# Segment attention of an eight-layer model on one core: probabilities turned one unit later, next batch's projections in quarters

## The reference, cut to what matters

```python
x = x + _L1_attn_a_ref(_layernorm(x), Wq, bq, Wk, bk, Wv, bv, Wo, bo)

def _L1_attn_a_ref(x, Wq, bq, Wk, bk, Wv, bv, Wo, bo):
    H, DK, SEG, NN, DIL = 16, 8, 64, 2, 4
    def _attn(q, k, v):
        scores = jnp.einsum('bshqd,bshkd->bshqk', q, k) / math.sqrt(q.shape[-1])
        return jnp.einsum('bshqk,bshkd->bshqd', jax.nn.softmax(scores, axis=-1), v)
    q, k, v = proj_chunk(Wq, bq), proj_chunk(Wk, bk), proj_chunk(Wv, bv)   # (batch, segment, head, 64, 8)
    out = _attn(q, k, v)
    kd, vd = k[:, :, :, ::DIL], v[:, :, :, ::DIL]
    for off in range(1, NN + 1):
        for sign in (-1, 1):
            n = seg_ids + sign * off
            valid, nc = (n >= 0) & (n < S), jnp.clip(n, 0, S - 1)
            out = out + jnp.where(valid, _attn(q, kd[:, nc], vd[:, nc]) / (2 * NN), 0.0)
    return merge_heads(out) @ Wo + bo
```

## Time and profile before

| what | value |
|---|---|
| median of 3 runs | 1274.57 us |
| lowest and highest | 1271.35 and 1275.83 us |
| profiled execution, its own time | 1270.62 us |
| its span, first to last instruction | 1268.9 us |
| segment stage in it, first maximum of unit 0 to that of unit 63 | 824.80 to 1067.97 us |
| VectorE, ScalarE, GpSimd busy over the whole span | 73%, 65%, 16% |
| mean granted clock of TensorE | 0.968 |

### The profile page before, as it was taken

One profiled execution on the slowest core, in us unless ns is written; L12 is line 12 of the kernel. 1 busy time (PEld: TensorE's weight loads), 2 busy tenths in 40 slices (PEclk: granted clock), 3 DMA queues, 4 the chain that ended last, 5 costly groups with the idle time before them and its releaser, 6 DMA issues.

```text
span 1268.9 us, 20399 instructions
## 1 busy us (share of the span) xinstructions
PE 1153.0 (91%) x7516; PEld 637.1 (50%) x7516; DVE 923.8 (73%) x1508; ACT 831.1 (65%) x1324; POOL 207.0 (16%) x313
## 2 busy tenths in 40 slices
PE   8988899999999999889998899798989888898787
PEld 4333344444444344367765353366666666463345
DVE  3869688777777756557775675488999997477766
ACT  5868655565565744745576636667787876768684
POOL 1000000000000000000000000167778777000000
PEclk9999999999999989979999999878999999999899
DMA  6000112212121000000000000000000000000002
GB/s 168 1 1 0 46 58 67 62 59 67 59 63 62 8 1 0 10 1 2 2 1 1 1 0 9 1 1 2 2 2 3 9 7 2 10 0 1 0 1 67
DMA packets 26076, 27.16 MB, mean 21 GB/s; under 512 B 3885, under 2 KB 17024, under 8 KB 25984
## 3 DMA queue, kind: packets, MB, share of 16 engines
q1 hardware_dynamic: 25938, 25.92, 6.9%
q10 hardware_dynamic: 46, 0.01, 0.0%
HBM read 23.30 MB, written 2.62 MB: 20 GB/s over the span
## 4 chain that ended last, share of the span: by engine, by line
PE 61%; DVE 16%; ACT 13%; issue 7%; POOL 1%; DMA 0%; DVEq 0%; ACTq 0%
PE psum L655 8%; PE psum L644 8%; PE psum L85 5%; PE psum L647 4%; PE psum L885 3%; PE psum L858 3%; PE psum L1830 3%; PE psum L1499 3%; ACT ln_std L112 3%; ACT ln_std L110 2%; PE psum L103 2%; PE psum L1273 2%; DVE arena L2010 2%; DVE N L2019 2%; ACT ln_sq L92 2%
## 5 line engine op out<-in xcount | busy, mean ns | idle before, releaser
L683 ACT ACTIVATE arena<-psum 128x512 f32<-128x512 f32 x128 | 69.5, 594 | 112.9 <-PE psum L644 112.9
L644 PE MATMUL psum<-arena,weights 128*128 128x512 f32 x256 | 120.8, 594 | 1.7 <-DVE N L124 1.0
L655 PE MATMUL psum<-arena,weights 128*128 128x512 f32 x256 | 120.3, 592 | 0.0
L103 PE MATMUL psum<-ln_sq,mean 128*128 128x512 f32 x192 | 97.1, 600 | 2.8 <-ACT ln_std L110 1.5
L541 DVE SCALAR_TENSOR_TENSOR arena<-diff,vecs,N 128x512 f32<-128x512 f32 x128 | 95.2, 746 | 0.0
L1930 ACT ACTIVATE N<-N 128x1024 f32<-128x1024 f32 x64 | 67.8, 1059 | 38.3 <-DVE N L2019 37.8
L603 DVE SCALAR_TENSOR_TENSOR arena<-arena,psum 128x512 f32<-128x512 f32 x64 | 44.0, 688 | 61.1 <-PE psum L655 61.1
L92 ACT ACTIVATE ln_sq<-psum 128x512 f32<-128x512 f32 x96 | 56.1, 593 | 45.5 <-PE psum L85 45.5
L1840 PE MATMUL psum<-ident,N 128*128 128x128 f32 x512 | 72.7, 287 | 12.5 <-POOL N L1983 11.9
L1830 PE MATMUL psum<-arena 32*128 32x128 f32 x1024 | 78.8, 295 | 4.8 <-ACT arena L1898 4.8
L1830 PEld LDWEIGHTS psum<-arena 32*128 32x128 f32 x1024 | 66.1, 197 | 31.3 <-issue 14.8
(11 more groups left out here) (318 smaller groups left out, 2452.2 us busy)
## 6 DMA issues: line engine op xcount, KB each, us to landing
arena<-tw_rows SPq DMA_DIRECT2D x64, 256.0 KB, 3.2
out_dram<-arena SPq DMA_DIRECT2D x8, 256.0 KB, 3.6
arena<-in_L_attn_a_x_dram SPq DMA_DIRECT2D x3, 512.0 KB, 6.4
weights<-in_L_attn_a_eWk_dram SPq DMA_DIRECT2D x1, 1024.0 KB, 5.9
arena<-in_L_attn_a_x_dram SPq DMA_DIRECT2D x2, 256.0 KB, 3.3
weights<-in_L_attn_a_eWr_dram SPq DMA_DIRECT2D x1, 512.0 KB, 9.6
tw_rows<-arena SPq DMA_DIRECT2D x2, 128.0 KB, 2.7
tw_rows<-arena SPq DMA_DIRECT2D x1, 256.0 KB, 3.7
```

What stands on the lines that cost most here:

```text
L103: self.nc.tensor.matmul(k.bank[W + c % self.vary][:], k.mean[:], k.ln_sq[:, c % W, :], start=True, stop=True).then_inc(k.ln_var, 1)
L644: op = nc.tensor.matmul(k.bank[2 * (n % 2) + h][:], k.eWk[:, e, h * P:(h + 1) * P], mixed[:, n % 4, 0, :], start=True, stop=True)
L655: op = nc.tensor.matmul(k.bank[4 + n % 2][:], k.eWv[:, e, h, :], ks[:, (2 * (n % 2) + h) * CH:(2 * (n % 2) + h + 1) * CH], start=(h == 0), ...
L683: op = nc.scalar.activation(kr[:, h * CH:(h + 1) * CH], k.bank[2 * (n % 2) + h][:], ACT.Relu)
```

## The change

- The transposes of the probabilities, on TensorE and ScalarE, come in iteration n-4 of a unit's own count instead of n-3 (that is `turned(n - 4)`), and the weighing follows as `weighed(n - 5)`. The loops run one iteration longer. The copy of finished heads, the output product and the addition come one position later.
- A projection is a quarter of a batch (256 columns): 12 for each next batch instead of 6, at positions 0, 1, 2, 3 (K), 4, 5, 7, 8 (V) and 10, 11, 12, 15 (Q). For a Q quarter ScalarE issues all four instructions, of 256 columns, in the same unit. Counts of `sg_kv` and `sg_q` follow.
- Values are transposed at positions 1, 5, 9 and 13, outputs made at 6 and 14.
- GpSimd's copies of neighbour keys and values move to positions 4 to 7 and 10 to 13.

```diff
--- before.py
+++ after.py
@@ -1777,19 +1777,20 @@
     def spread(v):
         return v.rearrange("p (h g) -> p h g", h=8)[:, :, :, None].to_broadcast([P, 8, 4, 16])
 
-    def own(v, b, c):
-        return v[b % 2][:, c * (NSEG // 2):(c + 1) * (NSEG // 2), 0:SEG]
-
-    PROJ = {0: 0, 1: 1, 3: 2, 4: 3, 7: 4, 11: 5}
+    def own(v, b, c, parts=2):
+        return v[b % 2][:, c * (NSEG // parts):(c + 1) * (NSEG // parts), 0:SEG]
+
+    PROJ = {0: 0, 1: 1, 2: 2, 3: 3, 4: 4, 5: 5, 7: 6, 8: 7, 10: 8, 11: 9, 12: 10, 15: 11}
+    QUARTER = L // 4
 
     def project_at(n):
-        return (n // 16 + 1) * 6 + PROJ[n % 16] if n < N - 16 and n % 16 in PROJ else None
+        return n // 16 * 12 + PROJ[n % 16] if n < N - 16 and n % 16 in PROJ else None
 
     def values_at(n):
-        return n // 4 if n < N and n % 4 == 2 else None
+        return n // 4 if n < N and n % 4 == 1 else None
 
     def output_at(n):
-        return (n - 13) // 8 if n >= 13 and n % 8 == 5 else None
+        return (n - 14) // 8 if n >= 14 and n % 8 == 6 else None
 
     @block.tensor
     def _(pe):
@@ -1807,16 +1808,16 @@
                                  start=True, stop=True).then_inc(k.sg_proj, 1)
 
         def project(p):
-            b, i = p // 6, p % 6
+            b, i = p // 12 + 1, p % 12
             free()
-            nc.tensor.matmul(other[:], k.sg_w[:, (1, 2, 0)[i // 2], :], k.Y[:, b * L + i % 2 * CH:b * L + (i % 2 + 1) * CH],
+            nc.tensor.matmul(other[:, 0:QUARTER], k.sg_w[:, (1, 2, 0)[i // 4], :], k.Y[:, b * L + i % 4 * QUARTER:b * L + (i % 4 + 1) * QUARTER],
                              start=True, stop=True).then_inc(k.sg_proj, 1)
-            last.append((k.sg_q, 4 * b + 2 * i - 6) if i >= 4 else (k.sg_kv, 4 * b - 4 + i + 1))
+            last.append((k.sg_q, 8 * b - 4 + 2 * (i - 7)) if i >= 8 else (k.sg_kv, 8 * b - 8 + i + 1))
 
         def scores(n):
             b, u, half = n // T2, n // 2, n % 2
             if n % T2 == 0:
-                pe.wait_ge(k.sg_q, 4 * b + 4)
+                pe.wait_ge(k.sg_q, 8 * b + 4)
                 pe.wait_ge(k.sg_kd, 4 * b + 4)
             if n < 2:
                 pe.wait_ge(k.sg_first, 2 * n + 2)
@@ -1871,13 +1872,13 @@
             last.append((k.sg_x, t + 1))
 
         first()
-        for n in range(N + 6):
+        for n in range(N + 7):
             if n < N:
                 scores(n)
-            if 0 <= n - 3 < N:
-                turned(n - 3)
             if 0 <= n - 4 < N:
-                weighed(n - 4)
+                turned(n - 4)
+            if 0 <= n - 5 < N:
+                weighed(n - 5)
             if project_at(n) is not None:
                 project(project_at(n))
             if values_at(n) is not None:
@@ -1893,20 +1894,21 @@
     def _(act):
         activations(act, k, "natural_log_exp_and_others")
 
-        def queries(src, b, c, part):
+        def queries(src, b, c, part, parts=2):
             for h in (2 * part, 2 * part + 1):
-                op = nc.scalar.activation(k.sg_Q[b % 2][:, c * (NSEG // 2):(c + 1) * (NSEG // 2), h, :], src.rearrange("p (s n) -> p s n", n=SEG),
+                op = nc.scalar.activation(k.sg_Q[b % 2][:, c * (NSEG // parts):(c + 1) * (NSEG // parts), h, :], src.rearrange("p (s n) -> p s n", n=SEG),
                                           ACT.Identity, bias=k.sg_qbias[:, h:h + 1], scale=k.sg_qscale[:, h:h + 1])
             op.then_inc(k.sg_q, 1)
 
         def project(p):
-            b, i = p // 6, p % 6
-            act.wait_ge(k.sg_proj, p + 1)
-            if i >= 4:
-                queries(other, b, i - 4, 0)
+            b, i = p // 12 + 1, p % 12
+            act.wait_ge(k.sg_proj, 6 + p + 1)
+            if i >= 8:
+                for part in range(2):
+                    queries(other[:, 0:QUARTER], b, i - 8, part, 4)
             else:
-                nc.scalar.activation(own((k.sg_K, k.sg_V)[i // 2], b, i % 2), other.rearrange("p (s n) -> p s n", n=SEG), ACT.Identity,
-                                     bias=k.vec(("bk", "bv")[i // 2])).then_inc(k.sg_kv, 1)
+                nc.scalar.activation(own((k.sg_K, k.sg_V)[i // 4], b, i % 4, 4), other[:, 0:QUARTER].rearrange("p (s n) -> p s n", n=SEG), ACT.Identity,
+                                     bias=k.vec(("bk", "bv")[i // 4])).then_inc(k.sg_kv, 1)
 
         def values(v):
             act.wait_ge(k.sg_vT, v + 1)
@@ -1946,19 +1948,17 @@
             act.wait_ge(k.sg_proj, 5 + c)
             for part in range(2):
                 queries(k.bank[4 + c], 0, c, part)
-        for n in range(N + 6):
-            if n >= 12 and n % 8 == 4:
-                heads((n - 12) // 8)
-            if 0 <= n - 3 < N:
-                turned(n - 3)
+        for n in range(N + 7):
+            if n >= 13 and n % 8 == 5:
+                heads((n - 13) // 8)
+            if 0 <= n - 4 < N:
+                turned(n - 4)
             if n < N:
                 exp(n)
             if 0 <= n - 1 < N:
                 weight(n - 1)
             if project_at(n) is not None:
                 project(project_at(n))
-            if project_at(n - 1) is not None and project_at(n - 1) % 6 >= 4:
-                queries(other, project_at(n - 1) // 6, project_at(n - 1) % 6 - 4, 1)
             if values_at(n) is not None:
                 values(values_at(n))
 
@@ -1990,12 +1990,12 @@
             around(k.sg_V, k.sg_vd, i, 0)
         for n in range(N):
             b, i = n // T2, n % T2
-            if n < N - T2 and 2 <= i < 6:
-                pool.wait_ge(k.sg_kv, 4 * b + 2)
-                around(k.sg_K, k.sg_kd, i - 2, b + 1)
-            if n < N - T2 and 7 <= i < 11:
-                pool.wait_ge(k.sg_kv, 4 * b + 4)
-                around(k.sg_V, k.sg_vd, i - 7, b + 1)
+            if n < N - T2 and 4 <= i < 8:
+                pool.wait_ge(k.sg_kv, 8 * b + 4)
+                around(k.sg_K, k.sg_kd, i - 4, b + 1)
+            if n < N - T2 and 10 <= i < 14:
+                pool.wait_ge(k.sg_kv, 8 * b + 8)
+                around(k.sg_V, k.sg_vd, i - 10, b + 1)
             halve(n)
             if n >= 1:
                 weigh(n - 1)
@@ -2044,8 +2044,8 @@
             if n < N:
                 maxima(n)
                 shift(n)
-            if n >= 14 and n % 8 == 6:
-                add((n - 14) // 8)
+            if n >= 15 and n % 8 == 7:
+                add((n - 15) // 8)
             if n >= 1:
                 sums(n - 1)
         add(TURNS - 1)
```

## The result

The changed kernel takes 1339.04 us (median of 4 runs, 1336.26 to 1340.95), that is 1.0508 times the kernel before (95% interval 1.0481 to 1.0535). The forecast was 1298 with a range of 1286 to 1311: the sign was right, and the size was less than half of what came. The profiled execution of the change spans 1339.0 us against 1268.9.

What follows compares the result with a forecast made beforehand. VectorE was taken to bound the segment stage, losing whatever time scores come late. Terms 5.6 + 17.2 - 2.1 - 1.3 = + 19.4, plus 4.5 for clock, on 1270.62 gave 1294.5, or 1298 against the median; range 1286 to 1311.

Steps and rivals of the forecast that it cites:

- What bounds the stage: Segment stage: VectorE bounds it, late scores are lost time; waits for scores grow from 20 to some 45 us.
- Double positions: Positions 1 and 5 hold a projection and the values on one PSUM bank: step 6.31, loss 2.87, twice a batch.
- the boundary: Position 15: the next batch's first scores wait for the last Q quarter, behind the addition: step 7.70, loss 4.26.
- The batch sum: Losses over one batch's positions: 15.5 us against 6.9 before, + 8.6, so + 17.2 for batches 1 and 2.
- The quarter's prices: A quarter projection costs TensorE 0.63 us; on ScalarE 0.45 per instruction, four Q instructions in one unit 1.80.
- The clock, + 4.5: Position 15: half a fall of TensorE's clock per batch from idling, 3.0 us a fall, 4.5 us in all.
- the harsher rival: Batches 0 to 2: the clock falls at each of nine places, 19.4 + 27, 1321 us; chance 0.10.
- Turning later: Transposes one unit later: the subtraction's new wait for them costs zero at full clock, some 0.5 per unit at half.
- Batch 3: Last batch, no projections: additions no longer stand before an event, so it gets 2.1 us faster.
- The - 1.3 at the end: Last weighing: centerings of the next norm that delayed it come one iteration earlier against it, saving 1.3 us.
- The faster rival: Segment stage: every event finds its slot and stalls but the eight additions go, 21.5 us less, 1253; chance 0.04.

Runs made afterwards that it cites:

- e1: The changed kernel plus TensorE products nobody reads, filling its waits at positions 1, 5, 7 and 15: 1304.69 us, 1.0224 times the kernel before.
- e2: The kernel before with turning one unit later alone, projections still halves, no position with two events: 1286.23 us, 1.0077 times the kernel before.
- e3: The changed kernel with turning later undone (transposes at n-3, weighing at n-4, copy of heads one position earlier), quarters kept: 1329.3 us, 1.0411 times the kernel before.

## Why the prediction was right and where it failed

- **What bounds the stage**: right. VectorE's own work is unchanged, and of the 67.3 us its waits for scores make 55 and the new wait for transposes 12. The waits for scores, forecast at some 45 us, came to 78.3; at nearly full clock, in e1, they are 53.5.
- **Double positions, 2.87 each, and the boundary, 4.26**: right within 0.11 us at full clock (e1: 6.29 and 7.81 against 6.31 and 7.70), and undoing them gave 35.5 and 25.8 us, clock losses included.
- **The batch sum, + 8.6**: right. e1's batch 1 shows + 8.9.
- **The quarter's prices**: right. TensorE's 0.63 holds (a quarter at 948.26, the scores behind it at 948.89; the step of position 7 is 5.16, as summed). Four Q instructions start at 962.43 in the change, and the next instruction of ScalarE, which did not wait, at 964.23: 1.80 us, as forecast. The Trainium skill's smaller fixed cost (Perfetto Trace Analysis, Optimizing Scalar/DVE Operations) would have made 1.43, as an estimate; the measurement decides for the dearer one.
- **The clock, + 4.5: this step failed.** I took half a fall per batch, at position 15, so 1.5 falls in all. In the change's trace the granted clock falls 15 times after the stage's start. Three falls lie at the boundary and five at positions 1 and 5. Five more lie behind the wait for the copy of the heads and two behind the wait for the addition at position 7; neither my term nor the harsher rival had those seven. The price of a fall, 3.0, was about right: what the stage lost beyond its waits is 67.3 - 27 = 40 us, 2.7 for each of 15. In batch 1 it cost 14.6 us, and batch 2 took the same 85.4 us. I had priced one wait at a time, each against the longest that seemed to have done no harm. Slow clock also makes the next steps late: position 0 by 1.6, and position 2 by 2.6 (6.08, where e1 has 3.45). Even the harsher rival (nine falls, 3.0 each) came to 1321, short of 1339.
- **The row under that term was misread.** I wrote that the other idle stretches of 1.77 us were followed by no fall. The stage before has seven of 1.76 or 1.77, each a wait for the addition. Six had no fall behind them; behind the last the transposes took 1.75 us instead of 1.09, and the clock from 1068 to 1070 was 0.53:

```profile
1066.17 0.66 PE L1863 MATMUL psum<-ident,arena 128*128 128x128 f32 x4 [1.77 <-DVE X L2033]
1066.76 1.16 PE L1830 MATMUL psum<-arena 32*128 32x128 f32 x16
1067.85 1.75 PE L1840 MATMUL psum<-ident,N 128*128 128x128 f32 x8
```

- **Turning later, nothing at full clock and 0.5 per unit at half**: near as a price (0.65 us, 19 times), but the weight was off, since I had it for the start alone. Two more terms were wrong. Batch 3, forecast at - 2.1, came to + 5.3. The - 1.3 at the end does not show: from the last first maximum to the end of the span are 202.0 us, against 200.9 before. I had treated TensorE's waits for GpSimd as free and removable. My reading is that they also spread its idle time, and that without them it bunches before the copy of the heads; slow scores follow there in the change and in e2. e3 prices turning later at 10 to 12 us.
- **The faster rival**, with the Trainium skill's rule that breaking up instructions may let work complete sooner (Perfetto Trace Analysis, Optimizing Scalar/DVE Operations): no run bears it out here. The pieces share one PSUM bank, and the doubles wait for that bank. The same page (Matmuls) wants independent groups to rotate through banks, so that taking one out overlaps the next. No run here gave the events a second bank, so what that would be worth is not shown.

The parts of the stage's 67.3 us: e1 keeps 275.6 - 243.2 = 32.4 of them, and its filler takes away 310.5 - 275.6 = 35, which is clock. Of the 32.4, waits make about 27, if batches 0 and 2 have the 8.9 of batch 1. The remaining 5 to 6 go with the three falls that e1 keeps and with its longer slow start (until about 848 in e1 and in the change, until about 840 before); this part was not measured by itself.

## What to carry to other kernels

When a chain of waits is made longer on a nearly full TensorE, price each wait twice: once as idle time, and once for the slow instructions that may follow it. Count all the waits of the new order, also those that were priced as small. A filler of unread products is a cheap experiment that tells waits and clock apart. Where one buffer serves many customers, look first at where its customers stand in their own queues: moving the addition ahead of four instructions of VectorE and the copy of the heads ahead of ScalarE's exponential gained 1.2%, without cutting anything smaller. And a wait that costs nothing may be what spreads an engine's idle time evenly, which these runs suggest but do not prove.

## What the runs showed of the hardware

A wait of some 2 us in one engine's queue can cost as much again behind it. The granted clock, full (2.4 GHz) over batch 1 of the kernel before, had a mean of 0.80 over the same batch of the change, so that two fifths of it ran at 1.2 GHz; with unread products in the same waits it was 1.00 again. Slow scores (2.08 us for 1.16) followed idle stretches of 1.95 us in the change (1095.95) and 2.26 us in e2 (946.93).

The length of one idle stretch does not decide it. Those of 1.77 us in the kernel before were followed by a fall once in seven times. In the change the same wait was followed by one here, where the scores ran at full speed and the transposes behind them did not:

```profile
948.26 0.70 PE L1813 MATMUL psum<-Y,weights 128*128 128x256 f32 x2 [1.77 <-DVE X L2033]
948.89 1.16 PE L1831 MATMUL psum<-arena 32*128 32x128 f32 x16
949.98 1.73 PE L1841 MATMUL psum<-ident,N 128*128 128x128 f32 x8
```

And of two stretches of 1.24 and 1.23 us in the kernel before, the one at 862.41 was followed by slow scores and the one at 1015.90 was not. What exactly decides, these runs do not show.
